# A two-layer decoder on one core: the next batch's softplus sums begun behind GpSimd's centring, and the softplus steps spread over the third attention's blocks

## What is computed

```python
x = x + L0_attn(ln(x))      # gated delta rule, 2 heads of 128, chunks of 64
x = x + L0_xattn(ln(x), ctx)  # 16 heads of 16, tanh layers ahead of q, k, v
x = x + L0_ffn(ln(x))       # 4 experts, top 2, hidden 512, inner layer norm
x = x + L1_attn(ln(x))      # 16 heads, causal, keys and values shared by the heads
x = x + L1_xattn(ln(x), ctx)  # 16 heads, causal mask
x = x + L1_ffn(ln(x))       # 8 experts, top 2, hidden 128
```

```python
log_decay = -exp(A_log) * softplus(einsum('btd,hd->bth', x, W_alpha) + dt_bias)
cum = cumsum(log_decay, -1)                  # within a chunk of 64
L_mask = tril(exp(tril(cum[..., :, None] - cum[..., None, :])))
```

## Time and profile before

| | |
|---|---|
| time, median of 3 runs (lowest, highest) | 5426.35 us (5419.66, 5430.18) |
| the profiled execution: time, span | 5424.35 us, 5421.6 us |
| granted TensorE clock, mean | 0.956 |
| PE, DVE, ACT, POOL busy | 86%, 77%, 43%, 74% of the span |
| load of x (512 KB), issue to landing, median | 3.6 us |

### The profile page before, as it was taken

The page is one execution under the profiler, slowest core; times in us unless marked ns, Lnnn a source line. Parts: engine busy times, 40 slices in busy tenths (PEclk is TensorE's granted clock), DMA queues, the critical chain, the costliest instruction groups (busy, mean ns, idle before and its releaser), DMA issues.

```text
span 5421.6 us, 105836 instructions
## 1 busy us (share of the span) xinstructions
PE 4688.4 (86%) x28201; PEld 3073.6 (57%) x28362; DVE 4177.1 (77%) x10963; ACT 2323.3 (43%) x4480; POOL 4005.8 (74%) x11220
## 2 busy tenths in 40 slices
PE   1059998999999899999989999898999999899998
PEld 1045664656566565656656565565656556565655
DVE  7068787787887778788787878778787887778788
ACT  0034444444444444444444444444444444444344
POOL 7878676786867678686767868677786867768686
PEclk7589999999999999999999999999999999999999
DMA  3000000000000000000000000000000000000000
GB/s 97 0 13 1 29 1 13 17 9 21 1 25 5 9 21 9 21 1 25 5 9 21 7 23 1 25 5 9 21 1 29 1 25 5 9 21 1 21 1 17
DMA packets 61879, 78.07 MB, mean 14 GB/s; under 512 B 11168, under 2 KB 53808, under 8 KB 61232
## 3 DMA queue, kind: packets, MB, share of 16 engines
q1 hardware_dynamic: 52784, 62.42, 3.5%
q10 hardware_dynamic: 8448, 8.39, 0.4%
HBM read 45.04 MB, written 8.46 MB: 10 GB/s over the span
## 4 chain that ended last, share of the span: by engine, by line
POOL 36%; PE 28%; DVE 17%; issue 11%; ACT 4%; POOLq 3%; DMA 0%; DVEq 0%; ACTq 0%; SPq 0%
POOL acc_c L584 12%; POOL arena L584 7%; POOL acc_a L584 3%; POOL acc_b L584 3%; PE bank L1280 3%; POOL acc_s L584 3%; POOL sl_t L584 3%; POOLq L583 3%; PE bank L1016 2%; DVE arena L2018 2%; PE bank L1187 2%; PE bank L1023 2%; PE bank L1140 2%; PE bank L1106 2%; ACT arena L779 2%
## 5 line engine op out<-in xcount | busy, mean ns | idle before, releaser
L1784 DVE TENSOR_REDUCE smax<-bank 128x4 f32<-128x512 f32 x768 | 524.4, 683 | 92.1 <-PE bank L1098 31.8
L766 ACT ACTIVATE arena<-bank 128x512 f32<-128x512 f32 x768 | 454.8, 592 | 248.4 <-PE bank L1106 242.6
L1788 DVE TENSOR_TENSOR arena<-bank,smax 128x512 f32<-128x512 f32 x768 | 530.8, 691 | 26.4
L1106 PE MATMUL bank<-ident,arena 128*128 128x128 f32 x3072 | 484.8, 280 | 45.1 <-ACT arena L753 28.1
L1092 PE MATMUL bank<-arena 64*128 64x512 f32 x1536 | 439.2, 648 | 64.4 <-ACT arena L790 28.0
L1187 PE MATMUL bank<-w,arena 128*128 128x512 f32 x1024 | 480.0, 599 | 14.0 <-DVE arena L1736 14.0
L1106 PEld LDWEIGHTS bank<-ident,arena 128*128 128x128 f32 x3072 | 345.7, 141 | 245.0 <-ACT arena L755 82.3
L1220 PE MATMUL bank<-w,arena 128*128 128x256 f32 x2048 | 454.1, 380 | 13.9 <-ACT arena L825 13.9
L753 ACT ACTIVATE arena<-arena,rstd 128x512 f32<-128x512 f32 x512 | 368.2, 719 | 201.4 <-DVE arena L1788 196.8
L1220 PEld LDWEIGHTS bank<-w,arena 128*128 128x128 f32 x2048 | 387.8, 190 | 90.3 <-issue 23.0
L584 POOL TENSOR_TENSOR acc_a<-acc_s,arena 128x32 f32<-128x32 f32 x1008 | 264.6, 262 | 171.6 <-DVE row L1347 47.2
(11 more groups left out here) (428 smaller groups left out, 11813.6 us busy)
## 6 DMA issues: line engine op xcount, KB each, us to landing
arena<-in_x_dram SPq DMA_DIRECT2D x35, 512.0 KB, 3.6
xn_next<-arena SPq DMA_DIRECT2D x17, 512.0 KB, 2.9
arena<-cum_dram SPq DMA_DIRECT2D x17, 512.0 KB, 3.6
arena<-in_ctx_dram SPq DMA_DIRECT2D x16, 512.0 KB, 3.7
out_dram<-arena ACTq DMA_DIRECT2D x16, 512.0 KB, 3.1
xn<-xn_next SPq DMA_DIRECT2D x15, 512.0 KB, 3.1
w<-in_L_ffn_w_dram SPq DMA_DIRECT2D x8, 512.0 KB
w<-in_L_ffn_w_dram SPq DMA_DIRECT2D x1, 1024.0 KB
```

The source lines that it names most:

```text
L766: act.activation(PT[:, v % 2], bank[3 + v % 2][:, :].rearrange("p (h q) -> p h q", h=QH), ACT.Copy).then_inc(S["pt"], 1)
L1106: ins = tr(bank[3 + v % 2][:, j * P:(j + 1) * P], Ssb[:, v % 4, j, :], ident[:, :])
L1784: dve.tensor_reduce(smax[:, u, :], sc, AX, ALU.max).then_inc(S["s_max"], 1)
L1788: dve.tensor_tensor(Ssb[:, u % 4], sc, smax[:, u, :].unsqueeze(2).broadcast_to([P, QH, P]), ALU.subtract).then_inc(S["s_sub"], 1)
```

## The change

On POOL, a new `chain_head` makes the 22 products of slice 0 and its first two groups (`HEAD_LINKS`) for the next iteration, once ahead of the loop and then in each iteration between `centered` and the wait for `y_ready`. It waits for `moved_next` of the next iteration. In the levels, groups 2 to 7 take the place of the products (two in level 1, none in level 2, one in each other), groups 8 to 12 stand behind the addition of line 601 (`NORM_LINKS`), 13 to 15 behind the reference's root; then the products of slice 1 and 13 groups (`ROUTER_LINKS`) ahead of the mixture's wait instead of five. `CHAIN_READ` goes from 530 to 587, and the wait for x_norm to the last group. `crow` goes to unit 16.

On DVE, `decay_exponential` takes a range of steps. In blocks 6 to 15 of the third attention part u - 6 is made, two steps between maximum and subtraction, the rest behind the subtraction; the wait for a step's end stands ahead of the next step, not behind it. Nothing of it is left behind the attention. `decay_remainder_sums` moves from behind the gates to ahead of them.

```diff
--- before.py
+++ after.py
@@ -179,7 +179,7 @@
         rk = cut(2, G * DH, P)
         rkT = sb("rkT", [P, DH, G, P + 1])
         ncol = sb("ncol", [P, G, DH])
-        crow = cut(24, G, DH, P)
+        crow = cut(16, G, DH, P)
         col = sb("col", [P, G, DH])
         off = sb("off", [P, DH, G, 2])
         jump = sb("jump", [P, DH, G])
@@ -573,21 +573,36 @@
             first_squares(0, 0)
             decay_table(0, 0)
 
+            src, linked = xn_next[:, :, :], [0]
+
+            def chain_head(it, a):
+
+                linked[0] = 0
+
+                def link(operation, *operands, known=False, behind=0):
+
+                    if linked[0] > behind and not known:
+                        pool.wait_ge(chain_step, nth(it, CHAIN_STEPS, linked[0] - behind, a))
+                    operation(*operands).then_inc(chain_step, 1)
+                    linked[0] += 1
+
+                pool.wait_ge(moved_next, nth(it, 16, 16, a))
+                chain_products(pool, link, src, 0)
+                chain_links(pool, link, 0, 0, HEAD_LINKS)
+
+            chain_head(0, 0)
+
             with nc.Fori(0, NIT, engines=[pool.engine], hint_back_edge=True) as it:
 
-                linked = [0]
-
                 def link(operation, *operands, known=False, behind=0):
 
-                    if linked[0] > behind and not known:
+                    if not known:
                         pool.wait_ge(chain_step, nth(it, CHAIN_STEPS, linked[0] - behind))
                     operation(*operands).then_inc(chain_step, 1)
                     linked[0] += 1
 
-                src = xn_next[:, :, :]
-                pool.wait_ge(moved_next, nth(it, 16, 16))
                 for l in range(1, LEVELS):
-                    chain_products(pool, link, src, 0, LEVEL_PRODUCTS[l - 1], LEVEL_PRODUCTS[l])
+                    chain_links(pool, link, 0, LEVEL_LINKS[l - 1], LEVEL_LINKS[l])
                     for h in range(DH):
                         if l == 1 and h == 0:
                             pool.wait_ge(S["inv_eye"], at(it, "inv_eye", 2))
@@ -600,11 +615,11 @@
                 pool.wait_ge(moved_now, nth(it, 16, 16))
                 pool.tensor_tensor(xres[:, :, :], xres[:, :, :], xn0[:, :, :], ALU.add).then_inc(S["xin_used"], 1)
 
-                chain_links(pool, link, 0, 0, 5)
+                chain_links(pool, link, 0, LEVEL_LINKS[LEVELS - 1], NORM_LINKS)
                 pool.wait_ge(S["xn"], at(it, "xn", 4))
                 pool.tensor_tensor(xres[:, :, :], xres[:, :, :], bo_row[:, :].unsqueeze(1).broadcast_to([P, G, D]), ALU.add).then_inc(S["bias_res"], 1)
                 pool.wait_ge(ref_step, nth(it, REF_STEPS, REF_BEFORE + ROOT_STEPS))
-                chain_links(pool, link, 0, 5, 16)
+                chain_links(pool, link, 0, NORM_LINKS, 16)
                 chain_products(pool, link, src, 1)
                 chain_links(pool, link, 1, 0, ROUTER_LINKS)
 
@@ -613,19 +628,18 @@
                 pool.wait_ge(S["g_w"], at(it, "g_w", 1))
                 chain_links(pool, link, 1, ROUTER_LINKS, 16)
                 chain_products(pool, link, src, 2)
-                chain_links(pool, link, 2, 0, 2)
-
-                chain_links(pool, link, 2, 2, 16)
+                chain_links(pool, link, 2, 0, 16)
                 chain_products(pool, link, src, 3)
-                chain_links(pool, link, 3, 0, 8)
+                chain_links(pool, link, 3, 0, 15)
                 pool.wait_ge(x_norm, nth(it, 1, 1, 2))
                 assert linked[0] < CHAIN_READ, linked[0]
-                chain_links(pool, link, 3, 8, 16)
+                chain_links(pool, link, 3, 15, 16)
                 chain_end(pool, link)
                 assert linked[0] == CHAIN_STEPS, linked[0]
                 pool.wait_ge(chain_step, nth(it, CHAIN_STEPS, CHAIN_STEPS))
                 pool.tensor_tensor(au[:, :], acc_a[:, :, 0], acc_a[:, :, 1], ALU.add).then_inc(au_ready, 1)
                 centered(it, 1)
+                chain_head(it, 1)
                 pool.wait_ge(y_ready, nth(it, 1, 2))
                 first_squares(it, 1)
                 decay_table(it, 1)
@@ -1453,50 +1467,63 @@
                 ins.then_inc(decay_step, 1)
                 dve.wait_ge(decay_step, nth(run["at"], DECAY_STEPS, run["decay"], run["d"]))
 
-            def decay_exponential(part):
+            def decay_exponential(part, first=0, last=4):
+
+                count = [0]
+
+                def dstep(operation, *operands, **named):
+
+                    if first <= count[0] < last:
+                        if run["decay"] > 0:
+                            dve.wait_ge(decay_step, nth(run["at"], DECAY_STEPS, run["decay"], run["d"]))
+                        operation(*operands, **named).then_inc(decay_step, 1)
+                        run["decay"] += 1
+                    count[0] += 1
 
                 if part == 0:
-                    dve.wait_ge(au_ready, nth(run["at"], 1, 1, run["d"]))
-                    dstep(tt(seqs(u[:, 0:SEQS]), seqs(au[:, :]), a_row[:, 1, :].unsqueeze(2).broadcast_to([P, DH, G]), ADD))
-                    dstep(stt(out=t[:, 0:SEQS], in0=u[:, 0:SEQS], scalar=-1.0, in1=u[:, 0:SEQS], op0=MUL, op1=ALU.min))
-                    dstep(ts(t[:, 0:SEQS], t[:, 0:SEQS], -86.0, None, ALU.max))
-                    dstep(dve.tensor_copy(t[:, SEQS:SEQS + DH], a_row[:, 0, :]))
+                    if first == 0:
+                        dve.wait_ge(au_ready, nth(run["at"], 1, 1, run["d"]))
+                    dstep(tt, seqs(u[:, 0:SEQS]), seqs(au[:, :]), a_row[:, 1, :].unsqueeze(2).broadcast_to([P, DH, G]), ADD)
+                    dstep(stt, out=t[:, 0:SEQS], in0=u[:, 0:SEQS], scalar=-1.0, in1=u[:, 0:SEQS], op0=MUL, op1=ALU.min)
+                    dstep(ts, t[:, 0:SEQS], t[:, 0:SEQS], -86.0, None, ALU.max)
+                    dstep(dve.tensor_copy, t[:, SEQS:SEQS + DH], a_row[:, 0, :])
                 if part == 1:
-                    dstep(ts(n_, t, 1.4426950408889634, 12582912.0, MUL, ADD))
+                    dstep(ts, n_, t, 1.4426950408889634, 12582912.0, MUL, ADD)
...
             def decay_quotient():
 
+                dve.wait_ge(decay_step, nth(run["at"], DECAY_STEPS, run["decay"], run["d"]))
                 dstep(ts(dh_, E, 2.0, None, ADD))
                 dstep(ts(x_, dh_, -2.0, None, ADD))
                 dstep(tt(x_, E, x_, SUB))
@@ -1782,24 +1809,22 @@
                             wait("s_psum", base + u + 1)
                             sc = bank[S_BANKS[u % 4]][:, :].rearrange("p (h k) -> p h k", h=QH)
                             dve.tensor_reduce(smax[:, u, :], sc, AX, ALU.max).then_inc(S["s_max"], 1)
+                            if a_no == 2 and 6 <= u:
+                                decay_exponential(u - 6, 0, 2)
                             wait("s_max", base + u + 1)
                             if u >= 4:
                                 wait("t_psum", base + u - 3)
                             dve.tensor_tensor(Ssb[:, u % 4], sc, smax[:, u, :].unsqueeze(2).broadcast_to([P, QH, P]), ALU.subtract).then_inc(S["s_sub"], 1)
                             if a_no == 1 and u % 2:
                                 exact_rest(1, u // 4, u // 2 % 2)
+                            if a_no == 2 and 6 <= u:
+                                decay_exponential(u - 6, 2, 4)
                         if u >= 6 and (u - 6) % 4 == 3 and (u - 6) // 4 < G:
                             b = (u - 6) // 4
                             if a_no == 1 and b == 2:
                                 exact_difference(1)
                             if a_no == 1 and b == 3:
                                 exact_last(1)
-                            if a_no == 2 and b == 2:
-                                for part in range(5):
-                                    decay_exponential(part)
-                            if a_no == 2 and b == 3:
-                                for part in range(5, 8):
-                                    decay_exponential(part)
                             wait("otr_psum", a_no * G + b + 1)
                             o = bank[7][:, :].rearrange("p (h d) -> p h d", d=2 * HD)
                             dve.reciprocal(orec[:, b, :], o[:, :, HD]).then_inc(S["o_rec"], 1)
@@ -1992,16 +2017,14 @@
 
                 layer_norm(5, xres, lambda m: add_y(2, 8, m))
                 xT_copy(5)
-                decay_exponential(8)
-                decay_exponential(9)
                 decay_quotient()
+                decay_remainder_sums()
                 wait("gl_psum", 1)
                 dve.tensor_copy(r_raw[:, :, :], bank[6][:, 0:G * E1].rearrange("p (g e) -> p g e", e=E1)).then_inc(S["g_ge"], 1)
                 wait("g_ge", 2)
                 gates(1, E1)
 
                 dve.tensor_tensor(gate[:, :, :], gsel[:, :, :], gsm[:, :].unsqueeze(2).broadcast_to([P, G, E1]), ALU.mult).then_inc(S["g_w"], 1)
-                decay_remainder_sums()
                 decay_remainder()
                 decay_series(0, 6)
```

(8 more changed lines are left out.)

48 lines of the change are left out of this document (24 added, 24 removed).

## The result

The changed kernel takes **5592.44 us** (median of 4 runs, 5590.22 to 5607.9) beside 5426.4 us for the kernel before: 1.0309 times as long, 95% interval 1.0294 to 1.0323. The profiled execution took 5590.22 us with a span of 5587.3, 165.7 us above the span before.

The account below looks back on a forecast made before the run. POOL, with its chain of softplus sums, held more than a third of the chain of waits. Terms: 16 x (6.5 + 1.0 - 0.9) + 20 = 126 us on 5424 gave 5550 us, range 5490 to 5615.

Parts of the forecast that it names:

- Once ahead of iteration 0: Before level 1 of iteration 0: 22 products and 25 links in place of four products, uncovered, +20 us once.
- First mixture: POOL's earlier products slow DVE's half 0 quotient and rests, so PE waits for expert 2: +6.5 us an iteration.
- Third attention: Softplus two by two and au in time gain, POOL's centring and products collide: +1.0 us an iteration.
- the -1.2 that I let ACT's queue absorb: Third attention: the last exponential already starts late, held by ACT's queue, which absorbs 1.2 us of the slowdown.
- Tail: Seven softplus steps leave it, y_nat comes earlier and PE's 0.87 us wait goes: -0.9 us an iteration.
- Levels: POOL's links in place of products in the levels are covered by its waits: no change.
- The head: Products and links behind the centring, 20 us on POOL, covered by its wait for y_nat: no cost.
- Rival 1: The collision in the first mixture does not reach PE, kernel not slower: 5398 us, chance 0.17.
- rival 2: Only the mixture collides, softplus in the attention is as good as hidden: 5502 us, chance 0.20.
- rival 3: Low bound of the mixture's loss, half the attention's gain: 5450 us or down to no difference, chance 0.11.
- rival 4: x_in arrives late and the head is not over before y_nat; 18 us more needed, no weight of its own.
- the signs that I named for "right": Profile signs: no au wait, y_nat wait 20 us or more, L1415 and L1423 near 0.8, PE's new 4 to 6 wait.

Follow-up runs that it names:

- rests_e2: Changed kernel with the eight rests of half 0's quotient moved from behind expert 1 to behind expert 2; 5458.51 us, 1.0041.
- late_centre: Changed kernel with one more wait on POOL: centring and head begin only after DVE's 34th softplus step; 5665.87 us, 1.0410.
- before_half: Kernel before with four of the eight rests (parts 2 and 3) moved behind expert 2, four left behind expert 1; 5433.77 us, 1.0013.
- old_time: Kernel before with the changed POOL code, its constants and crow in unit 16, but ROUTER_LINKS = 5 in place of 13; 5580.88 us, 1.0262.
- pool_only: Kernel before with the changed kernel's POOL code, its constants and crow in unit 16, DVE's code as before; 5605.82 us, 1.0314.
- before_rests: Kernel before with all eight rests of half 0's quotient moved from behind expert 1 to behind expert 2; 5415.54 us, 0.9967.

## Why the prediction was right or wrong

The sign, the size and the main step held: 5550 forecast, 5592 measured, inside the range. By its own steps:

- **Once ahead of iteration 0, +20.** Measured 21 to 23 us in all eight executions with a head. Level 1 begins at 347.53, where the last product ahead of it ended at 324.42. Right.
- **First mixture, +6.5.** Measured +7.0, of which rests_e2 takes back 6.6. The products come eight groups of links, 64 operations, earlier; the head makes 31 of these, and the other 33 come from the levels and the stretch up to the norm, where eleven groups of links stand in place of 22 products and five groups. The rests cost 2.8 us more (2.5 forecast), the quotient 2.0 (2.5), PE's wait is 5.00 us and the lower clock behind it 1.6 (1.1). Right, term by term. By the rule of the Trainium skill (SBUF — State Buffer, Who interferes with whom) at its word the whole would have been near 5604 us; the measured 5592 seems to speak for it, but the rows don't: a rest takes 6.97 / 8 = 0.87 us, not 0.53 + 0.73.
- **Third attention, +1.0.** Measured +2.7 over both attentions, 2.3 of it in the third. This is the first mis-sized term. Without any collision late_centre gives -1.4 (I had -2.0). The products add 3.5 (2.9), the centring 0.7 (1.3). Nothing shows the -1.2 that I let ACT's queue absorb: -1.4 + 0.7 + 3.5 is already the whole. That step failed.
- **Tail, -0.9.** Measured -1.1 up to y_nat and -0.7 behind it. The second part I did not have: in 5 of 15 iterations before, the stretch behind y_nat took 20.3 us instead of 18.0, and the changed kernel has none of these.
- **Levels, 0.** Measured -0.35.
- **Keys and queries, not in the sum.** +1.3 on the mean, 20 us in all: 11.6 to 12.0 us in 10 of 15 iterations at the lower clock, 7.70 in the others. This is the missing term. Its five iterations at 7.70 us take 325.1 us on the mean, the ten others 328.6. Moving the rests removes it in nearly all iterations that were profiled, in both kernels, so it is tied to DVE's and PE's order in the mixture; by which mechanism stays open, since before_half has neither the wait nor full clock.
- **The head: "Cost: none, as long as the wait for y_nat stands."** In the tail this is true of the changed kernel, only because the head is over (1604.6) before DVE's tail begins; in the attention the head's products cost 3.5 us. late_centre and old_time show the same head costing 7.8 and 8.7 us with POOL's wait still standing.

Rival 1 (no collision at PE) is refuted by the wait of 5.00 us, rival 2 by the softplus steps at 0.5 us and more, rival 3 by the mixture's size, rival 4 (the head comes too late) by its end at 1604.6, well ahead of y_nat. Of the signs that I named for "right" all are there but one: the first quotient's L1415 (now L1429) takes 1.08 / 2 = 0.54 us, not near 0.8.

The number owes a little to luck: third attention and keys together came out 3.0 us an iteration above the sum, and tail and levels 1.3 us below it, for the greater part without a reason that I had given.

What the change gives and takes, by the runs: its softplus part gives nothing in the changed kernel itself (pool_only is level with it) and 1.9 to 3.4 us an iteration with the rests moved; the earlier au by itself gives nothing (pool_only); the moved products take 6.6 us an iteration in the mixture, and 9.4 with the keys' clock in the best execution. With the rests moved the changed kernel's iteration is 317.5 us there, 1.1 below before; at its median it is nearer 319.3 (the estimate above), level with before, and the 21 us of iteration 0 come on top. No version is clearly ahead of the kernel before: before_rests is by 0.2 to 0.3%, and I take it as evidence on the clock, not as a kernel to use.

## What to carry to other kernels

A wait on GpSimd's side hides GpSimd's work only for GpSimd. If DVE is the one that makes the awaited result, out of small dependent steps, work put into that wait slows it down; look at what DVE does beside it before calling it free. When a long GpSimd chain is shifted, list what each of its wide operations newly lies beside: here one DVE block of 7 us, already just in time, carried most of the loss, and moving its rests one expert on cured it. Bursts and spread steps should be compared with the neighbour that they will have, not the one that they had. Where the clock of PE varies, a stage that got faster is counted only together with the stages behind it, and a profiled execution is first set beside the median of its kernel.

## What the runs showed of the hardware

- GpSimd's 128x256 products slow DVE's SBUF operations by amounts that depend on their size: 256-wide scalar_tensor_tensor 0.53 to 0.87 us, 512-wide tensor_tensor 0.69 to 1.10, 128x8 steps 0.17 to about 0.6 every second time. The products themselves take 0.79 us beside the rests and 0.72 behind them (changed kernel, 1790.33 to 1801.20). DVE's reduce and subtract on PSUM banks stay at 0.68 and 0.69 beside them.
- A joint of PE can fall to the lower clock (0.50) without any new wait in it: 3.76 us for 1.96 at the queries. The same program shows 7.7 us and 11.9 us for this joint in neighbouring iterations of one execution, whose iterations take 324 to 330 us. A single iteration is therefore no measure. The mean of 15 is better, but it can miss too: rests_e2's profiled execution lies 30 us below the median of its kernel.
- Time at the lower clock moves between stages: in pool_only keys and queries at 7.7 us instead of 11.8 come with an attention of 91.1 us instead of 88, and the iteration takes 328.1 us instead of 327.3 to 327.9.
